# A fused pair of Swin blocks: banks for the attends, 128-row tables on Scalar's queue, queries and keys in three products, new instruction orders

## The reference, cut to what matters

```python
h = roll(ln1(x), (-3, -3)); h -> windows of 7 x 7 = 49 tokens
q, k, v = split(h @ qkv_w + qkv_b)
attn = softmax((q * hd ** -0.5) @ k.T + rel_bias + shift_mask)   # 49 x 49 for each head
o = (attn @ v) @ proj_w + proj_b;  x = x + roll_back(o)
m = gelu(ln2(x) @ fc1_w + fc1_b)          # 96 -> 384
m = ln3(m)                                # block 0 only
x = x + m @ fc2_w + fc2_b                 # 384 -> 96
```

## Time and profile before

| | |
|---|---|
| median of the runs | 7013.29 us |
| profiled execution | 7008.9 us, span 7007.0 us |
| PE busy | 6744.4 us, 96% of the span |
| ACT busy | 5480.9 us, 78% |
| DVE busy | 5000.4 us, 71% |
| POOL busy | 4518.2 us, 64% |
| DMA | 327 MB moved, mean share of the 16 DMA engines about 18% |
| granted TensorE clock | mean 0.994 of full speed |

### The profile page before, as it was taken

The page is one execution under the profiler, slowest core; times in us unless marked ns, Lnnn a source line. Parts: engine busy times, 40 slices in busy tenths (PEclk is TensorE's granted clock), DMA queues, the critical chain, the costliest instruction groups (busy, mean ns, idle before and its releaser), DMA issues.

```text
span 7007.0 us, 283199 instructions
## 1 busy us (share of the span) xinstructions
PE 6744.4 (96%) x97326; PEld 5658.6 (81%) x97326; DVE 5000.4 (71%) x18724; ACT 5480.9 (78%) x11268; POOL 4518.2 (64%) x4612
## 2 busy tenths in 40 slices
PE   0899999999999999999999999999999999999999
PEld 0688888888888888888888888888888888888887
DVE  0577777777777777777777777777777777777776
ACT  0588888888888888888888888888888888888887
POOL 0466666666666666666666666666666666666665
PEclk9899999999999999999999999999999999999999
DMA  0111111111111111111111111111111111111111
GB/s 30 38 48 47 50 47 46 49 47 47 49 47 47 48 47 48 47 48 49 47 47 49 47 47 49 47 47 49 47 47 49 47 48 48 47 49 47 48 49 37
DMA packets 604323, 327.23 MB, mean 47 GB/s; under 512 B 449870, under 2 KB 603856, under 8 KB 604048
## 3 DMA queue, kind: packets, MB, share of 16 engines
q1 hardware_dynamic: 604274, 326.57, 17.9%
HBM read 82.32 MB, written 38.54 MB: 17 GB/s over the span
## 4 chain that ended last, share of the span: by engine, by line
PE 78%; DVE 14%; issue 4%; SPq 2%; DVEq 1%; POOL 0%; ACT 0%; DMA 0%; ACTq 0%; POOLq 0%
PE ps L394 19%; PE ps L542 16%; PE ps_o L483 12%; PE ps L507 6%; PE ps L430 5%; PE ps L420 5%; DVE negmax L833 4%; PE ps L451 3%; PE ps L520 3%; DVE shifted L837 3%; PE ps L412 3%; PE ps L549 2%; SPq L285 2%; DVE bnM L808 2%; PE ps L521 2%
## 5 line engine op out<-in xcount | busy, mean ns | idle before, releaser
L671 ACT ACTIVATE probsT<-ps 98x392 f32<-98x392 f32 x2048 | 872.9, 491 | 631.7 <-PE ps L394 605.1
L935 POOL TENSOR_TENSOR rstdA<-var_epsA,minus_half 98x4 f32<-98x4 f32 x512 | 515.4, 1007 | 1314.4 <-DVE var_epsA L816 1314.4
L837 DVE TENSOR_TENSOR shifted<-ps,negmax 113x392 f32<-113x392 f32 x2048 | 1160.7, 567 | 212.9
L833 DVE TENSOR_REDUCE negmax<-ps 113x8 f32<-113x392 f32 x2048 | 1142.8, 558 | 22.0 <-PE ps L451 22.0
L688 ACT ACTIVATE hid<-ps,bfc 128x392 f32<-128x392 f32 x1536 | 876.4, 587 | 218.0 <-PE ps L523 213.9
L656 ACT ACTIVATE ps<-table 113x392 f32 (+1 forms) x2048 | 957.3, 494 | 57.5 <-DVE shifted L837 2.0
L664 ACT ACTIVATE probs<-shifted 113x392 f32<-113x392 f32 x2048 | 941.6, 520 | 8.1 <-DVE shifted L837 5.2
L394 PE MATMUL ps<-ident,probs 113*98 113x113 f32 x8192 | 938.6, 263 | 2.3 <-ACT probsT L671 1.7
L483 PEld LDWEIGHTS ps_o<-vM,probsT 98*49 98x49 f32 x32768 | 793.7, 125 | 105.2 <-issue 64.6
L483 PE MATMUL ps_o<-vM,probsT 98*49 98x50 f32 (+1 forms) x32768 | 851.4, 201 | 0.3 <-DVE o_norm L848 0.3
L394 PEld LDWEIGHTS ps<-ident,probs 113*98 113x98 f32 x8192 | 806.0, 130 | 11.1 <-ACT probs L664 3.4
(11 more groups left out here) (98 smaller groups left out, 14221.3 us busy)
## 6 DMA issues: line engine op xcount, KB each, us to landing
kM<-kT SPq DMA_DIRECT2D x512, 85.8 KB
vM<-vA SPq DMA_DIRECT2D x1024, 41.3 KB
vM<-vA SPq DMA_DIRECT2D x1024, 38.3 KB
x_in<-in_x SPq DMA_DIRECT2D x256, 147.0 KB
x_again<-in_x SPq DMA_DIRECT2D x256, 147.0 KB
kM<-kT SPq DMA_DIRECT2D x1024, 36.8 KB
x_keep<-x_next SPq DMA_DIRECT2D x256, 147.0 KB
out_y<-y_out SPq DMA_DIRECT2D x256, 147.0 KB
```

The lines of the kernel that those rows point to most:

```text
L671: act.activation(probsT[:, unit_buffer(L, u), :, :, :], free(ps[bank_of[f"T{L}{u}"]][0:PT, 0:1], (SP, 4), (64, 2), (1, TOK)), ACT.Copy).th ...
L833: dve.tensor_reduce(negmax[:, buf, :], s, AX.X, ALU.max, negate=True).then_inc(s_mx[L], 1)
L837: dve.tensor_tensor(shifted[:, buf, :].rearrange("p (h k) -> p h k", k=TOK), s, free(negmax[:, buf, 0:1], (1, 8), (0, TOK)), ALU.add).then ...
L935: pool.tensor_tensor(rstd[n][:, :], var_eps[n][:, :], minus_half[:, :], ALU.pow).then_inc(s_rstd[n], 1)
```

## The change

**The setup.** `table`, `shifted` (through which `t_in` is loaded) and their DRAM sources have 128 rows in place of 113; the rows between and behind the two halves are zeros. The three loads (bias, mask of ordinary strips, mask of last-row strips) are issued on ACT's queue with a semaphore of their own, `s_tables`, on which only DVE waits, just ahead of the additions. The two small DMAs of the bias rows move to ACT's queue too.

**Queries and keys.** `q` and `k` use the three products of `fc1`, through a common helper. ACT writes the high part `xqT_high` beside `xnT` (which `v` still reads), so `turned` has two activations in place of one for the first norm of each block. A new DVE step `low_part_qk` makes the low part. The setup gets six more DVE operations that split the weights.

**Banks.** The fixed bank `ps_o` is gone: all eight banks are in `BANKS`, `o0` has bank 7 and `o1` bank 6.

**Orders.** The `body` of SP, PE, ACT, DVE and POOL is new. Block 0's second half (M0 and its fc1) works on strip i - 1 in place of i - 2; block 1's residual and M1 statistics on i - 3 in place of i - 4. The number of iterations is the same.

```diff
-        table = sb("table", [SP, 2 * NT])
+        table = sb("table", [128, 2 * NT])
...
+        tables = [(t_in, d["tab"])] + [(table[:, v * NT:(v + 1) * NT], d["mask"][:, v * NT:(v + 1) * NT]) for v in (0, 1)]
+        loads = [(ident[:, :], d["ident"])]
...
+            for dst, src in tables:
+                act.dma_start(dst, src).then_inc(s_tables, 16)
+            act.wait_ge(s_w, NW_BROW)
+            for L in (0, 1):
+                act.dma_start(wqkv[L][C:C + 1, :], brow[L][0:1, :]).then_inc(s_brow, 16)
...
+            def three(out, w_high, w_low, x_high, x_low, low_ready):
+                pe.matmul(out, w_high, x_high, start=True, stop=False)
+                pe.matmul(out, w_low, x_high, start=False, stop=False)
+                pe.wait_ge(*low_ready)
+                return pe.matmul(out, w_high, x_low, start=False, stop=True)
...
             def q(x, L):
-                    pe.wait_ge(s_xe[f"A{L}"], x.count(1, 1))
+                    pe.wait_ge(s_xh[L], x.count(1, 1))
...
-                    pe.matmul(ps[bank_of[f"q{L}"]][0:QK[L], 0:ST], wqkv[L][:, 0:QK[L]], xnT[L][:, :], start=True, stop=True)\
-                      .then_inc(s_q[L], 1)
+                    three(ps[bank_of[f"q{L}"]][0:QK[L], 0:ST], wqk_high[L][:, 0:QK[L]], wqk_low[L][:, 0:QK[L]],
+                          xqT_high[L][:, :], xqT_low[L][:, :], (s_ql[L], x.count(1, 1))).then_inc(s_q[L], 1)
...
+                    act.activation(xqT_high[L][0:C, :], g, ACT.Copy).then_inc(s_xh[L], 1)
                     act.activation(xnT[L][0:C, :], g, ACT.Copy).then_inc(s_xe[n], 1)
...
+            def low_part_qk(x, L):
+                if x.exists(ns):
+                    dve.wait_ge(s_xe[f"A{L}"], x.count(1, 1))
...
+                    dve.tensor_tensor(xqT_low[L][0:C, :], ps[bank_of[f"xtA{L}"]][0:C, 0:ST], xqT_high[L][0:C, :].bitcast(f32),
+                                      ALU.subtract).then_inc(s_ql[L], 1)
...
+        BANKS = [("sc10", 3, 0), ("sc11", 3, 3), ("sc12", 3, 4), ("f2_1", 5, 5), ("sc00", 1, 1), ("sc01", 1, 2),
+                 ("f2_0", 2, 0), ("T00", 1, 1), ("sc13", 3, 4), ("sc14", 3, 3), ("sc15", 3, 5), ("T01", 1, 2),
...
+                 ("xtA1", 2, 0), ("q0", 0, 3), ("T15", 3, 4), ("f1_0_1", 4, 5), ("k1", 2, 2), ("f1_1_1", 4, 4),
```

More of the change, by code:

```diff
@@ L264, in swin_program @@
                       (rows[L][:, :], d[f"rows{L}"]), (wproj[L][:, :], d[f"wproj{L}"])]
-        NCONST = 16 * len(loads)
-        NMEMSET, NW_BROW, NW = 12, 4, 21
+        NCONST, NTABLES = 16 * len(loads), 16 * len(tables)
+        NMEMSET, NW_BROW, NW = 13 + len(O_BANKS), 4, 27
         def iterate(eng, body):
@@ L386, in _ @@
             pe.wait_ge(s_brow, 32)
-            for bank in ps[:7]:
-                mm = pe.matmul(bank[:, 0:4 * SP], ident[:, :], free(ident[:, 0:1], (0, 4), (1, SP)), start=True, stop=True)
+            for n in range(8):
+                if n in O_BANKS:
+                    continue
+                mm = pe.matmul(ps[n][:, 0:4 * SP], ident[:, :], free(ident[:, 0:1], (0, 4), (1, SP)), start=True, stop=True)
             mm.then_inc(s_wps, 1)
@@ L646, in table_of @@
                     start = (1 if x.i - x.off >= last_row_from else 0) * NT + col
-                    return table[:, start:start + UNIT_COLS]
+                    return table[0:SP, start:start + UNIT_COLS]
                 which = (x.i + (256 - last_row_from - x.off)) // 256
-                return table[:, bass.ds(which * NT + col, UNIT_COLS)]
+                return table[0:SP, bass.ds(which * NT + col, UNIT_COLS)]
             def seed(x, L, u):
@@ L795, in _ @@
                 done(dve.tensor_tensor(table[:, half], table[:, half], t_in, ALU.add))
+            dve.wait_ge(s_brow, 32)
+            for L in (0, 1):
+                done(dve.tensor_copy(wqk_high[L][:, :], wqkv[L][:, 0:2 * QK[L]]))
+                done(dve.scalar_tensor_tensor(out=wqk_low[L][:, :], in0=wqk_high[L][:, :].bitcast(f32), scalar=-1.0,
+                                              in1=wqkv[L][:, 0:2 * QK[L]], op0=ALU.mult, op1=ALU.add))
+                done(dve.tensor_copy(xqT_high[L][C:C + 1, :], xnT[L][C:C + 1, :]))
             assert step[0] == NW
@@ L914, in body @@
                 shift(s3, 1, 2)
+                shift(s1, 0, 0)
                 finish1(s5)
+                shift(s1, 0, 1)
+                third_stats(s2)
                 shift(s3, 1, 3)
+                finish0(s2)
+                normalise(s1, 0)
+                stats(s2, "A1")
                 shift(s3, 1, 4)
+                low_part_qk(s0, 0)
                 shift(s3, 1, 5)
+                residual(s1, 0)
                 low_part(s4, 1)
-                third_stats(s2)
-                finish0(s2)
-                stats(s2, "A1")
+                stats(s1, "M0")
+                low_part_qk(s2, 1)
                 normalise(s3, 1)
-                normalise(s1, 0)
+                low_part(s1, 0)
+                residual(s3, 1)
+                stats(s3, "M1")
             iterate(dve, body)
```

200 lines of the change are left out of this document (100 added, 100 removed), and 10 rows, old and new, of the table BANKS.

## The result

The changed kernel takes 7486.93 us (median of four runs, 7470.16 to 7505.75) against 7014.86 us before (7011.72 to 7017.15) on the same chip: ratio 1.067, 95% interval 1.064 to 1.071. It is slower; 6725 had been predicted. The profiled execution took 7470.16 us, 7468.2 of them in the span.

The account below looks back on a forecast made before the run. PE, busy 96%, was taken to bound the loop, after a setup waiting on slow table loads. 7007.0 - 150 (setup) - 138 (loop) = 6719 of span, 6725 on the median's scale; 8-in-10 range 6620 to 6865.

Parts of the forecast that it names:

- waits that come: In the loop, DVE's fuller line makes PE wait before block 1's fifth transposes and just behind: 0.2 us per iteration, bounds 0 to 0.8.
- sum of DVE's line: DVE's work from block 1's residual to its last unit of scores: 17.9 us, against 17.7 for PE to `T14`.
- The rival on the slower side: POOL's in-order squares, norms and roots run late, holding DVE and then PE: period 27.2, 7082 us; chance 0.05.
- Setup: Before the loop, 128-row loads bring the first matmul from 168.8 to 16 us: -150 us, bounds -135 to -155.
- Queries and keys: On PE, four sets of three products replace four fp32 products: 0.14 us gained per iteration, bounds +0.20 to -0.48.
- Period 25.8: Loop iteration forecast: 25.6 us plus 0.2 of new waits, down from 26.34; 138 us off over 255 iterations.
- PE at its own pace: Rival: DVE's line is shorter and the sets cost less; period 25.5, 6649 us; chance 0.19.
- Signs of being wrong: PE waiting mainly for POOL or ACT, lone sets costing 0.6 or less, early DMA share under 0.1.
- Attends in three blocks: On PE, one more change between transposes and attends costs 0.1 us per iteration, bounds 0 to 0.2.
- waits that go: On PE, bank waits at block 0's third fc1 chunk and at `q1` vanish: 0.67 us per iteration, bounds 0 to 0.67.

Follow-up runs that it names:

- experiment 5: Kernel before plus one spare 98x4 DVE `tensor_scalar`, read by nobody, placed where POOL runs its squares: 7290.16 us, ratio 1.040.
- experiment 10: Kernel before plus the same spare DVE `tensor_scalar` behind `finish0(s2)`, where POOL runs no squares: 7015.19 us, ratio 1.000.
- experiment 6: Changed kernel with epsilon added by a DVE `tensor_tensor` whose two inputs are both in SBUF: 7150.06 us, ratio 1.020 to the kernel before.
- experiment 7: Changed kernel, complete, with epsilon added by a DVE `tensor_tensor` with one input in PSUM: 6745.26 us, ratio 0.962 to the kernel before.
- experiment 2: Changed kernel plus eight spare fp32 matmuls of 64 columns in PE's wait before the transposes of probabilities: 7106.56 us, ratio 1.013 to the kernel before.
- experiment 1: Changed kernel without DVE's epsilon step, epsilon left out of the norms A and M: 6616.2 us, ratio 0.943 to the kernel before.
- experiment 3: Changed kernel with POOL's squares in three instructions of 392 columns instead of one of 1176: 6757.75 us, ratio 0.964 to the kernel before.
- experiment 4: Kernel before with only the new setup (tables of 128 rows, on ACT's queue): 6865.33 us, ratio 0.979.
- experiment 12: Kernel of experiment 7 with queries and keys as single fp32 matmuls again, without the added copies and low parts: 6772.1 us.
- experiment 11: Kernel of experiment 7 without DVE's epsilon step in both A norms: 6593.12 us with POOL adding epsilon, 6589.73 with it left out.

## Why the prediction was wrong

**The step that failed** is the one on waits that come, in its sum of DVE's line: it took the statistics of A0 and A1 at 2 x 1.29, a duration read where POOL did not square, and put A0's in a place where it did. There they take 2.77 us (513.45 to 516.22), 1.48 more. Put into the prediction's own line, that makes its 25.8 into 27.3; 27.23 was measured at full clock. The rule "a duration from a row holds after a move" does not hold for an instruction that shares something with what another engine runs at the new place. The 2.15 us of squares were in view, and both new orders too; that the two would overlap could have been asked of them, though the orders alone do not give the times. The rival on the slower side had POOL hold up DVE, but through data that come late, by a line of waits from squares to roots; what holds DVE up needs no data of POOL's. The Trainium skill states this in "SBUF — State Buffer", section on who interferes with whom: DVE and GpSimd share a pair of ports, one instruction has it to its end, and the other blocks; `tensor_scalar` has a mode that takes it; an instruction with two inputs in SBUF contends with a GpSimd instruction that reads SBUF; a `tensor_tensor` with only one SBUF input does not contend. Experiments 5 and 10, 6 and 7 agree (1568 and 159 ns; 895 and 158 ns in the mean). This rule spoke against the change, and it was not weighed.

**The clock was no term at all.** The trace of before has a clock of 0.994, and the sum has nothing for a change of it, without a reason given. It made half of the 762 us between forecast and measurement: 383 us. The Trainium skill has a case like it in "TensorE: Matmul & The Clock Gate", "HAM oscillation — how this bites in real kernels": there a wait for DMA in each pass of a loop takes PE's clock down again. The rows here agree in so far as the slow stretch starts 1.2 us behind the wait of 1.14 us (clock record at 767.8), and as the clock stays where the wait is filled (experiment 2) or gone (1, 3 and 7). It does not explain experiments 5 and 6, whose waits are as long and whose clock holds or nearly so.

**The sum, with both put in.** From experiment 7, which has the whole change without the hold-up: 6745. Hold-up: (27.23 - 25.87) x 255 = 347. Clock: (28.73 - 27.23) x 255 = 383. Together 7475; the median is 7487, and the profiled execution, from which the periods are read, took 7470. The two differences are measured on the changed kernel itself, so this shows that nothing else is missing; it is no test of the causes.

**The other terms, by the runs without the hold-up:**
- *Setup*, -150 predicted: -144.7 in the changed kernel up to the first 1x1 matmul, -149 in experiment 4. The first matmul came at 22.5 instead of 16, within the bounds; the tables moved at the rate of this window, DMA share 0.83 in place of 0.08. The rows and the queue were changed together, so no run tells what the move to ACT's queue gave:

```profile
2.00:22.00 20.00, 0.00 (x0) 0.00 (x0) 6.18 (x11) 0.00 (x0) 0.00 (x0) 1.00 0.83 298
```

- *Queries and keys*, -0.14 per iteration: experiment 12 has 0.14. That it fits so well is partly luck: it is measured where DVE holds PE up, and by the starts below the four sets take 2.35 us, 0.29 less than the four fp32 products. The sets on PE, by starts:

```profile
531.30 0.41 PE L416 MATMUL ps<-xqT_high,wqk_high 97*112 97x392 f32 x1
531.55 0.34 PE L417 MATMUL ps<-xqT_high,wqk_low 97*112 97x392 f32 x1
531.73 0.34 PE L419 MATMUL ps<-xqT_low,wqk_high 97*112 97x392 f32 x1
531.90 0.55 PE L401 MATMUL ps<-ident,probs 113*98 113x113 f32 x4
```

  A lone set takes 0.60 (531.30 to 531.90), not 0.71; the ones next to a chunk of `fc1` take 0.53 and 0.62.
- *Period 25.8*: 25.87 in experiment 7, with the epsilon step not held up. The mechanism is the one forecast: PE waits at `T14` for DVE's last unit, 0.3 us against 0.2. That the sum fits to 0.07 is luck, since two errors cancel. PE's own work was put at 25.6, and experiments 1 and 11 have 25.37 and 25.27 (the rival *PE at its own pace* had 25.5); the waits that DVE's line causes were put at 0.2 and are 0.6.
- *Signs of being wrong*: two of the prediction's own came. PE waits mainly for ACT (325 us in front of the transposes of probabilities), and a lone set costs 0.60.
- *Attends in three blocks* (+0.1) and the *waits that go* (-0.67) were not tried apart. Only their sum with the rest is shown, by the period of experiment 11.

**What stays open:** what decides whether the clock falls. Shown is that the clock's part of the loss comes with the hold-up (experiments 1, 3 and 7 have neither), that a little more work on PE, inside the wait or outside, shortens the wait and nearly ends it, and that a later place of A0's statistics makes it worse. But with the full wait experiment 6 keeps nearly all of the clock, and no run tells why. Of the 0.6 us that 158 ns twice cost in DVE's line, 0.44 are seen in DVE's starts and the rest is not.

## What to carry to other kernels

When an instruction of DVE moves, look at what POOL runs at its new place, however small the instruction is, and use a `tensor_tensor` with one input in PSUM, move the step to POOL, or split POOL's long instruction (experiments 7, 11 and 3; the squares in three take 0.28 us more). When PE gets a wait once per iteration, its clock is a term of the sum; and an instruction of 0.16 us in a full line should be counted by the starts of its neighbours (0.22 us here). A duration carries over to another kernel only together with its neighbours.

## What was not expected of the hardware

- A 98x4 `tensor_scalar` in fp32 is held to the end of a POOL `tensor_tensor` of 2.15 us, at 0.17 us of its own.
- PE's clock fell to 1.2 GHz again and again in a loop in which PE is busy for 95% of the time, and two matmuls of 64 columns more per iteration gave back 5% of the kernel's time (7487 to 7109 and 7102). Without them and with the same wait, the clock of experiment 6 fell 12 times in the loop in place of 55.
- A `tensor_tensor` that adds 98x4 elements takes 0.20 us on POOL, while the one that takes a power of as many takes 1.01.
